# Causal self attention: the second score pass as matmuls on a quarter of the array's rows

## The reference, cut to what matters

```python
for l in range(N_LAYERS):
    h = rmsnorm(x, n1[l])
    qkv = h @ Wqkv[l].T + bqkv[l]
    q, k, v = jnp.split(qkv, 3, axis=-1)
    q = apply_rope(split_heads(q, H), cos, sin)
    k = apply_rope(split_heads(k, H), cos, sin)
    o = merge_heads(sdpa(q, k, split_heads(v, H), causal_bias)) @ Wo[l].T + bo[l]
    x = x + o
    ...
```

## Time and profile before

| | |
|---|---|
| median of 3 runs | 2466.01 us |
| the profiled execution, its own time | 2462.31 us |
| its span | 2460.5 us |
| granted TensorE clock, mean | 0.946 |
| PE busy | 2116.1 us, 86% |
| DVE busy | 1524.0 us, 62% |
| ACT busy | 1065.8 us, 43% |
| POOL busy | 540.3 us, 22% |
| k_self DMAs | 256, 64 KB each, 2.0 us to landing |

### The profile page before, as it was taken

The page is one execution under the profiler, slowest core; times in us unless marked ns, Lnnn a source line. Parts: engine busy times, 40 slices in busy tenths (PEclk is TensorE's granted clock), DMA queues, the critical chain, the costliest instruction groups (busy, mean ns, idle before and its releaser), DMA issues. The chain is left out here.

```text
span 2460.5 us, 33327 instructions
## 1 busy us (share of the span) xinstructions
PE 2116.1 (86%) x12714; PEld 1310.3 (53%) x12714; DVE 1524.0 (62%) x3596; ACT 1065.8 (43%) x1424; POOL 540.3 (22%) x756
## 2 busy tenths in 40 slices
PE   6978999799773899899898899889889988989977
PEld 4556665466541455565554565545556555556553
DVE  7546654544866666764566674467675457666468
ACT  4543555222351355554254556244545434545510
POOL 1111001000123334210244220234320034421020
PEclk9988999899986899999999999999999989999988
DMA  4001000000000000000000000000000010000000
GB/s 154 13 1 52 1 12 1 14 1 1 1 1 11 22 19 21 9 9 11 26 22 18 18 10 1 28 22 18 23 5 9 1 31 18 23 13 10 1 1 17
DMA packets 25614, 41.16 MB, mean 17 GB/s; under 512 B 8168, under 2 KB 13680, under 8 KB 24816
## 3 DMA queue, kind: packets, MB, share of 16 engines
q1 hardware_dynamic: 25456, 39.03, 5.5%
HBM read 21.19 MB, written 1.05 MB: 9 GB/s over the span
## 5 line engine op out<-in xcount | busy, mean ns | idle before, releaser
L1483 DVE TENSOR_REDUCE maxima<-wide 128x4 f32<-128x1024 f32 x256 | 312.4, 1223 | 230.4 <-PE wide L613 229.9
L1704 ACT ACTIVATE prob<-wide 128x1024 f32<-128x1024 f32 (+2 forms) x384 | 325.6, 881 | 157.7 <-PE wide L613 157.5
L1633 ACT ACTIVATE prob<-wide 77x1024 f32<-77x1024 f32 x256 | 260.0, 1018 | 156.1 <-PE wide L613 154.7
L1166 DVE TENSOR_REDUCE maxima<-wide 128x8 f32<-128x616 f32 x256 | 203.5, 796 | 179.3 <-PE wide L613 177.3
L1875 POOL TENSOR_SCALAR_AFFINE_SELECT prob<-prob 128x256 f32<-128x256 f32 (+1 forms) x384 | 185.4, 488 | 522.8 <-ACT prob L1704 522.8
L613 PE MATMUL wide<-k_self,q_g 128*128 128x512 f32 x640 | 256.9, 482 | 33.4 <-DMA k_self<-q_g 29.2
L1576 ACT ACTIVATE q_g<-acc 128x512 fp32r<-128x512 f32 x192 | 114.5, 597 | 374.6 <-PE acc L613 374.1
L613 PE MATMUL wide<-q_g,k_self 128*128 128x512 f32 (+3 forms) x1024 | 245.8, 352 | 28.1 <-ACT prob L1704 14.8
L1757 POOL TENSOR_TENSOR rstd<-moments,cst 128x4 f32<-128x4 f32 x88 | 89.7, 1020 | 784.6 <-DVE moments L1056 347.5
L613 PE MATMUL wide<-q_g,kx 128*77 128x512 f32 x512 | 257.1, 574 | 5.3 <-DVE hid L1398 2.0
L613 PE MATMUL acc<-prob,A 128*32 128x512 f32 (+3 forms) x2048 | 197.3, 444 | 35.7 <-POOL prob L1875 35.3
(11 more groups left out here) (217 smaller groups left out, 3439.9 us busy)
## 6 DMA issues: line engine op xcount, KB each, us to landing
k_self<-q_g SPq DMA_DIRECT2D x256, 64.0 KB, 2.0
A<-in_w SPq DMA_DIRECT2D x2, 2048.0 KB, 12.5
...
```

The source lines that it names most:

```text
L1166: e.tensor_reduce(maxima[g % 2][:, 2 * half:2 * half + 2, :], v, AX.X, ALU.max, negate=True).then_inc(*made("max", ("free", tile)))
L1483: e.tensor_reduce(top[:, at0, :], s.rearrange("p (c i k) -> p i c k", c=2, i=HG), AX.XY, ALU.max, negate=True).then_inc(*made("max", ("fre ...
L1633: e.activation(p[0:SC, :], s[0:SC, :], ACT.Exp, bias=0.0, scale=1.0).then_inc(*made("exp", pb, ("free", tile)))
L1704: e.activation(pv, sv, ACT.Exp, bias=0.0, scale=8 ** -0.5).then_inc(*made("exp", pb, ("free", tile)))
```

## The change

The second score pass no longer reads `k_self`. It takes the 32 rows of head i from q_g itself for both operands, k from [:, 1] and q from [:, 0], so a matmul uses a quarter of the array's rows, the four heads use four different quarters, and head i and i + 1 of a tile write two different banks. The last two blocks of keys (j = 2 and 3) are now two tiles of two heads, each holding 256 columns for j = 2 and 128 for j = 3 in one bank, in place of one tile for j = 2 and one for j = 3 with four heads each: again six tiles. `k_self` is released after the fifth causal_max and has two buffers, so the start writes 8 pieces of zeros on ACT and not 12. The rows of the order are new: both tiles of a block of keys stand in one row (3, 5, 7), and the causal_max steps stand in rows 0, 1, 4, 6, 8. The two prob buffers of j = 2 and 3 are both released by values(3).

```diff
--- before.py
+++ after.py
@@ -255,12 +255,12 @@
         return rows
 
     def scores(b, g):
-        return in_rows(*[(row, ("causal_max", l, b, g, k)) for k, row in enumerate((0, 1, 3, 5, 7))])
+        return in_rows(*[(row, ("causal_max", l, b, g, k)) for k, row in enumerate((0, 1, 4, 6, 8))])
 
     def attend(b, g):
         logits, values = (lambda j, h0: ("self_logits", l, b, g, j, h0)), (lambda j: ("self_values", l, b, g, j))
-        return in_rows((1, ("self_full", l, b, g)), (3, logits(0, 0)), (4, logits(0, 2)), (5, logits(1, 0)),
-                       (6, logits(1, 2)), (6, values(0)), (7, logits(2, 0)), (8, logits(3, 0)), (8, values(1)),
+        return in_rows((1, ("self_full", l, b, g)), (3, logits(0, 0)), (3, logits(0, 2)), (5, logits(1, 0)),
+                       (5, logits(1, 2)), (6, values(0)), (7, logits(2, 0)), (7, logits(2, 2)), (8, values(1)),
                        (9, values(2)))
 
     def finish(b, g):
@@ -371,7 +371,7 @@
         k_tok = A[:, 0:2048].rearrange("p (t h r) -> p t h r", t=NI, h=16)
         v_self = bufs("v_self", 2, lambda n: A[:, 1536 * n + 2048:1536 * n + 3584].rearrange("p (t c) -> p t c", t=NI))
         y = A[:, 6144:8192].rearrange("p (t d) -> p t d", t=NT)
-        k_self = bufs("k_self", 3, lambda n: sb(f"k_self{n}", [P, HG, S], FR))
+        k_self = bufs("k_self", 2, lambda n: sb(f"k_self{n}", [P, HG, S], FR))
         unit_w = bufs("unit_w", 2, lambda n: sb(f"unit_w{n}", [P, U_W]))
         att_w = bufs("att_w", 1, lambda n: sb("att_w", [P, L_ATT]))[0]
         ffn_w = bufs("ffn_w", 1, lambda n: sb("ffn_w", [P, L_FFN]))[0]
@@ -472,10 +472,10 @@
             five = [k[:, W * n:W * n + W].rearrange("p (i e) -> p i e", e=E8) for n in range(5)]
             return *five, k[:, 5 * W:5 * W + NI], k[0:E8, S:2 * S]
 
-        def self_tile(j, h0):
-
-            per, n = HG if j > 1 else 2, S - P * j
-            return per, n, n if j > 1 else S
+        def self_tile(j):
+
+
+            return (S - P * j, S - P * j) if j < 2 else (3 * P, S)
 
         def head_at(g, i):
 
@@ -878,7 +878,7 @@
                     i_mm = mm(bank, q[:, P * t:P * t + P], kk[:, :, P * j:P * j + P], stop=t != j)
                     if t == j:
                         i_mm = mm(bank, ident_b[:, :], causal_b[:, :].unsqueeze(1).broadcast_to([P, HG, P]), start=False)
-                i_mm.then_inc(*made("scores", tile))
+                i_mm.then_inc(*made("scores", tile, *([("free", ("sk", l, b, g))] if k == len(CAUSAL_TILES) - 1 else [])))
 
             def self_full(l, b, g):
                 tile = ("sq_full", l, b, g)
@@ -890,15 +890,15 @@
 
             def self_logits(l, b, g, j, h0):
                 tile = ("slogits", l, b, g, j, h0)
-                s = wide[T.slot("wide", tile)]
-                q, kk = q_g[T.slot("q_g", ("sq", l, b, g))][:, 0, :], k_self[T.slot("k_self", ("sk", l, b, g))]
-                per, n, pitch = self_tile(j, h0)
+                s, qk = wide[T.slot("wide", tile)], q_g[T.slot("q_g", ("sq", l, b, g))]
                 for w in need(T.freed("wide", tile), ("sq_filled", l, b, g)):
                     e.wait_ge(*w)
-                for i in range(h0, h0 + per):
-                    at0 = pitch * (i - h0)
-                    i_mm = mm(s[:, at0:at0 + n], kk[:, i, P * j:P * j + P], q[:, P * j:S])
-                ends = [("free", ("sq", l, b, g)), ("free", ("sk", l, b, g))] if j == NI - 1 else []
+
+                for jj in (j,) if j < 2 else (2, 3):
+                    for i in (h0, h0 + 1):
+                        r, at0 = slice(HR * i, HR * i + HR), S * (i - h0) + (S // 2 if jj == 3 else 0)
+                        i_mm = mm(s[:, at0:at0 + S - P * jj], qk[r, 1, P * jj:P * jj + P], qk[r, 0, P * jj:S])
+                ends = [("free", ("sq", l, b, g))] if (j, h0) == (2, 2) else []
                 i_mm.then_inc(*made("logits", tile, *ends))
 
             def self_values(l, b, g, j):
@@ -909,15 +909,15 @@
                     for w in need(T.freed("acc", tile), ("vs", l, b)):
                         e.wait_ge(*w)
                 ends = []
+                (_, pitch), at_key = self_tile(min(j, 2)), 2 * P if j == 3 else 0
                 for i in range(HG):
-                    per, n, _ = self_tile(j, 0)
-                    h0 = i // per * per
-                    pb = ("sprob", l, b, g, j, h0)
-                    if i == h0:
-                        ends.append(("free", pb))
-                        for w in need(("scaused", l, b, g, j, h0)):
+                    pb = ("sprob", l, b, g, min(j, 2), i // 2 * 2)
+                    if i % 2 == 0:
+                        ends += [("free", pb)] if j != 2 else []
+                        for w in need(("scaused", *pb[1:])):
                             e.wait_ge(*w)
-                    p = prob[T.slot("prob", pb)][:, n * (i - h0):n * (i - h0) + n]
+                    at1 = pitch * (i % 2) + at_key
+                    p = prob[T.slot("prob", pb)][:, at1:at1 + S - P * j]
                     at0 = head_at(g, i)
                     i_mm = mm(a[HR * i:HR * i + HR, P * j:S], vs[:, j, at0:at0 + HR], p, start=(g % 2, j) == (0, 0),
                               stop=last)
@@ -1565,7 +1565,7 @@
 
             for w in need(("blank",)):
                 e.wait_ge(*w)
-            for n in range(3 * HG):
+            for n in range(2 * HG):
                 e.activation(k_self[n // HG][:, n % HG, :], small[:, 0:1].broadcast_to([P, S]), ACT.Copy, bias=0.0,
                              scale=1.0).then_inc(*made("begin", ("begun", "act")))
             for w in need(("const",), ("small",), ("begun", "dve"), ("begun", "pool")):
@@ -1696,9 +1696,9 @@
             def self_logits(l, b, g, j, h0):
                 tile, pb = ("slogits", l, b, g, j, h0), ("sprob", l, b, g, j, h0)
                 s, p = wide[T.slot("wide", tile)], prob[T.slot("prob", pb)]
-                per, n, pitch = self_tile(j, h0)
-                sv = s[:, 0:pitch * per].rearrange("p (i k) -> p i k", i=per)[:, :, 0:n]
-                pv = p[:, 0:n * per].rearrange("p (i k) -> p i k", i=per)
+                n, pitch = self_tile(j)
+                sv = s[:, :].rearrange("p (i k) -> p i k", i=2)[:, :, 0:n]
+                pv = p[:, 0:2 * pitch].rearrange("p (i k) -> p i k", i=2)[:, :, 0:n]
                 for w in need(tile, T.freed("prob", pb)):
                     e.wait_ge(*w)
                 e.activation(pv, sv, ACT.Exp, bias=0.0, scale=8 ** -0.5).then_inc(*made("exp", pb, ("free", tile)))
@@ -1868,11 +1868,12 @@
 
             def self_logits(l, b, g, j, h0):
                 pb = ("sprob", l, b, g, j, h0)
-                per, n, _ = self_tile(j, h0)
-                v = prob[T.slot("prob", pb)][:, 0:n * per].rearrange("p (i k) -> p i k", i=per)[:, :, 0:P]
+
+                every, many = (self_tile(j)[1], 2) if j < 2 else (2 * P, 4)
+                v = prob[T.slot("prob", pb)][:, 0:every * many].rearrange("p (i k) -> p i k", i=many)[:, :, 0:P]
                 for w in need(pb):
                     e.wait_ge(*w)
-                e.affine_select(out=v, in_=v, compare_op=ALU.is_ge, fill=0.0, base=0, pattern=[[0, per], [1, P]],
+                e.affine_select(out=v, in_=v, compare_op=ALU.is_ge, fill=0.0, base=0, pattern=[[0, many], [1, P]],
                                 channel_multiplier=-1).then_inc(*made("causal", ("scaused", l, b, g, j, h0)))
 
             def m_add(b):
```

## The result

| | before | after |
|---|---|---|
| median | 2465.34 us (4 runs, 2462.85 to 2466.13) | 2556.6 us (4 runs, 2551.46 to 2558.14) |
| ratio | | 1.0368, 95% interval 1.035 to 1.0386 |
| profiled execution, own time | 2462.31 us | 2556.08 us |
| its span | 2460.5 us | 2554.4 us |
| granted TensorE clock, mean | 0.946 | 0.907 |

A forecast was written before the change was run, and what follows sets the result against it. The prediction took a chain through PE, ACT and DVE over three wide tiles as the bound, so PE's saving becomes waiting; plain 2, project 25, layer-end 4, rotate and merge 6 make 37 us more: 2503 us, range 2455 to 2545.

The forecast's parts named there:

- What bounds the kernel: Plain round: a chain over three wide tiles through PE, ACT and DVE; PE is busy but mostly not what ends last.
- the rival in which PE is the bound: Waits exist only because PE is late; each item gains 0.7 us: 2421 us, or 2443 with half the rounds; chance 0.13.
- What PE saves: Second score pass: four quarters run as one, 0.64 us an item against 2.55, so 1.9 us less PE work.
- The rival of quarters that don't run together: Quarters run not together or only two together: 0.2 to 0.3 us more in most rounds, 2519 us; chance 0.1.
- What PE pays: Six changes of tiling per item at 0.2 us each: 1.2 us if none is hidden, 0 if all are.
- the sum: Plain 2, project 25, layer-end 4, rotate and merge 6: 37 us more, giving a median of 2503 us.
- Plain round: All the saving becomes waiting behind the third maximum tile; plus 0.1 us in each of 16 rounds.
- Project round: o_norm waits behind the third maximum on DVE and delays the first qkv step; plus 2.1 us in each of 12 rounds.
- The four rounds of this kind at the layers' ends: Rounds like the project round but without a qkv step; taken at plus 1.0 us each, 4 us in all.
- The sentence that the granted clock of the rounds below 0.95: Sign against the forecast: it is wrong if the granted clock of the rounds falls below 0.95.
- Rotate and merge: values(3)'s wait for POOL goes, but the last causal_max moves behind cut_q on DVE; plus 0.35 us for both rounds together.
- a rival of chance 0.25 and 28 us: The clock falls to 1.2 GHz once in each of 28 project and merge rounds: 28 us more, 2531 us; chance 0.25.

The follow-up runs named there:

- own_order: The changed kernel with the maxima back in rows 0, 1, 3, 5, 7 and the logits in rows 3, 3, 5, 6, 6, 7; 2464.8 us.
- full_array: The changed kernel, its order and two-head tiles kept, with full-array score matmuls on k_self (three buffers) in place of quarters; 2516.9 us.
- quarters_01: The kernel before, order and cut untouched, with quarter tiles for the logits of keys 0 to 255 only; 2491.4 us.

## Why the prediction was wrong

**What bounds the kernel: right.** Nearly all that PE saved became waiting, and the rival in which PE is the bound found nothing: no order came out faster with quarters than without them.

**What PE saves: right in kind.** The 512-wide quarters are busy 45.2 us, just beyond the 25 to 45 that were named. The rival of quarters that don't run together falls: in the plain round four of them, of 494 ns mean, take 0.57 us from the first start to the last end.

**What PE pays** by changes of tiling was not measured by itself and was in no part of the sum. In rounds that keep a clock of 1.00, those with quarters are at most 0.1 us longer than the same rounds without, and mostly shorter (in own_order's order 12.17, 16.89, 13.41 and 11.81 us against 12.26, 16.93, 13.46 and 12.39), so what the changes cost is about made up for by what the quarters save.

**Plain round: right.** The third maximum stands 3.16 us behind the second (875.11 against 871.95; forecast 3.2), values(0) 5.25 us into the round (forecast 5.3), the round 12.27 (forecast 12.2).

**Project round: the chain right, its length not.** Counted from the round's start: third maximum filled at 4.5 (forecast 4.8), o_norm at 7.0 (6.7), first qkv step at 7.9 (7.7, and 6.1 before). Then the clock: the step takes 2.92 us, the next maximum pair 1.48, and values(0) comes at 11.4 where 9.6 was forecast. The round takes 20.86 in place of 19.3. At a clock of 1.00, with the full array, the same order takes 18.56, so the chain adds 1.4 us to it and not 2.1, and the clock does the rest. The four rounds of this kind at the layers' ends were taken at 1.0 us each: they rise from 14.15 to 15.51 with the full array at 1.00, and to between 17.3 and 19.1 in the change. The sentence that the granted clock of the rounds below 0.95 would prove the forecast wrong is what happened (0.84 and 0.88).

**Rotate and merge: mis-sized.** The term was 0.35 us for both. At a clock of 1.00, in full_array, they take 14.36 and 13.25, which is 1.06 more than before. The 0.9 us by which the last maximum pushes the next round's second maximum were seen in the forecast; that the merge round catches up most of it was wrong. That is 16 x 0.7 = 11 us. In the change itself the merge round loses another 0.5 us to the clock.

**The step that failed** is the sum, where it sets the clock's cost to nothing and puts it into a rival of chance 0.25 and 28 us. It is no alternative to the chain; it comes on top of it, and it was priced too low. Chain and cut measured 52 us with the full array (forecast 37), the quarters 40 (forecast 0 in the likeliest case). The 52 hold some 8 us of PE's own time in the plain rounds (12.78 against 12.27), which the quarters save, and the 40 are what the clock costs less such savings. The argument against the rival, that PE is never idle long, stayed true and proved nothing: before the clock fell, PE's longest wait was 0.65 us in the change's project round and 0.22 us in quarters_01's plain round. Nor is the project round always the first to lose its clock, as the forecast had it: in quarters_01, from 1262 to 1379 us, the plain and rotate rounds lost it, and the two project rounds between them kept it (17.11 us at 1.00). The forecast's row at the first layer's start did show a stretch of PE work at 0.62 behind an emptier one, and it should have carried more than a quarter of the chance. The Trainium skill (TensorE: Matmul & The Clock Gate, section Part 1: The HAM clock gate) has the slow clock as the default that activity lifts; by that rule a change that takes PE's work away from a chain that PE does not bound can lose its clock, and the trace agrees: 213 us at 1.2 GHz with the quarters, 44 without them, in one and the same order.

**What the forecast did not separate:** cut and order. They give 15 and 39 us, and of the 39 the third maximum's one row is 36. The rows of the change are no bad answer to its own cut: with the old rows the split tile's select costs 30 us on POOL (full array).

**What stays open:** what in the quarters lowers the clock, and when. The pairs show that putting them in does it. Whether it is the smaller work of all, or that a matmul on 32 rows uses less of the array while it counts as just as busy, no run separates; nor why quarters_01 loses its clock in two layers and keeps it in the other two. The quarters cost 40, 38, 28, 20, 17 and 7 us in six pairs of kernels, with some 170, 94, 69, 102, 53 and 45 us more at 1.2 GHz; the two go together, but not in proportion, since the quarters also shorten rounds and the clock can fall where PE waits anyway. A variant that keeps the quarters and the clock together was not found.
